# Attention: how the sums over the values are divided and brought into the order of the last layer

## The reference

```python
x = x + 0.5 * ffn(layernorm(x))
x = x + attention(layernorm(x))
x = x + 0.5 * ffn(layernorm(x))

def attention(x):                       # 16 heads of 16 features, scale = 16 ** -0.25
    xd = (x @ W_down).reshape(b, t, 16, 16)
    keys, queries = (einsum('bthk,hik->bthi', xd, w) * scale for w in (tokeys, toqueries))
    values = einsum('bthk,hik->bthi', xd, tovalues)
    attn = softmax(einsum('bqhs,bkhs->bhqk', queries, keys), axis=-1)
    out = einsum('bhqk,bkhs->bqhs', attn, values).reshape(b, t, 256)
    return out @ W_unify + b_unify
```

## Time and profile before

| | us |
|---|---|
| median of 3 runs | 2948.91 (2944.68 to 2953.52) |
| profiled execution, its own time | 2942.43 |
| its span in the profile | 2940.3 |
| TensorE busy | 2753.6 (94%) |
| VectorE busy | 2133.7 (73%) |
| ScalarE busy | 1863.4 (63%) |
| GpSimd busy | 539.7 (18%) |
| mean granted TensorE clock | 0.968 of full |

### The profile page before, as it was taken

How to read it: one execution, slowest core, us unless ns; L and a number is a source line. 1 busy time by engine, 2 the same in 40 slices (tenths; PEclk the granted TensorE clock), 3 DMA queues, 4 the chain that set the end, 5 groups by cost and what they waited for, 6 DMA issues and landing times. The chain is left out here.

```text
span 2940.3 us, 49181 instructions
## 1 busy us (share of the span) xinstructions
PE 2753.6 (94%) x17263; PEld 1663.3 (57%) x17263; DVE 2133.7 (73%) x3460; ACT 1863.4 (63%) x3505; POOL 539.7 (18%) x498
## 2 busy tenths in 40 slices
PE   5999999867999999999999999999999679999997
PEld 3799998853334343333343443333433369999886
DVE  6554456748888888898898888888897465445664
ACT  5444455634777777777777777777777454544564
POOL 3354124520000000000000000000000145421353
PEclk9999999977999999999999999999999889999998
DMA  5221113415033132131230330321220412111242
GB/s 170 65 57 43 43 59 113 130 38 89 15 58 69 25 65 47 38 60 36 48 73 15 59 67 23 67 45 37 47 43 8 149 47 72 52 48 43 89 140 66
DMA packets 159668, 180.69 MB, mean 61 GB/s; under 512 B 31816, under 2 KB 129296, under 8 KB 159504
## 3 DMA queue, kind: packets, MB, share of 16 engines
q1 hardware_dynamic: 151312, 167.99, 23.4%
q0 software_dynamic: 8192, 10.57, 1.2%
HBM read 96.46 MB, written 30.49 MB: 43 GB/s over the span
## 5 line engine op out<-in xcount | busy, mean ns | idle before, releaser
L1518 DVE TENSOR_REDUCE at_mxc<-at_pb 128x2 f32<-128x1024 f32 x1024 | 1222.7, 1219 | 159.6 <-PE at_pb L1335 152.0
L1448 ACT ACTIVATE at_ex<-at_pd 128x512 f32<-128x512 f32 x2048 | 1092.9, 598 | 355.0 <-PE at_pd L1346 346.4
L768 DVE TENSOR_TENSOR f_ml_hl<-f_ml_h,f_ml_hh 128x512 fp32r<-128x512 f32 (+1 forms) x384 | 265.2, 692 | 441.1 <-ACT f_ml_hh L844 382.8
L1346 PE MATMUL at_pd<-at_qa,at_ka 50*128 50x512 f32 x2048 | 573.4, 466 | 3.3 <-ACT at_ex L1448 2.5
L1346 PEld LDWEIGHTS at_pd<-at_qa,at_ka 50*128 50x128 f32 x2048 | 255.8, 185 | 526.9 <-issue 271.3
L1355 PE MATMUL at_po<-at_ex,at_va 128*32 128x512 f32 x4096 | 547.1, 606 | 0.2 <-ACT at_ex L1448 0.2
L841 ACT ACTIVATE f_ml_h<-f_ml_pL,b1T 128x512 f32<-128x512 f32 (+1 forms) x384 | 243.6, 634 | 449.9 <-PE f_ml_pL L895 373.6
L1335 PE MATMUL at_pb<-at_ka,at_qa 48*128 48x512 f32 x2048 | 441.8, 450 | 16.0 <-DVE at_mxc L1518 10.7
L910 PE MATMUL f_ml_pA<-f_wh,f_ml_hh 128*128 128x256 f32 (+1 forms) x1408 | 408.8, 290 | 0.0
L912 PE MATMUL f_ml_pA<-f_wl,f_ml_hh 128*128 128x256 f32 (+1 forms) x1408 | 401.3, 285 | 0.0
L913 PE MATMUL f_ml_pA<-f_wh,f_ml_hl 128*128 128x256 f32 (+1 forms) x1408 | 401.3, 285 | 0.0
(11 more groups left out here) (124 smaller groups left out, 2658.9 us busy)
## 6 DMA issues: line engine op xcount, KB each, us to landing
f_wraw<-in_L_ffn_w SPq DMA_DIRECT2D x128, 256.0 KB, 2.7
at_qa<-at_parts SPq DMA_DIRECT2D x384, 64.0 KB, 2.4
at_ka<-at_parts SPq DMA_DIRECT2D x384, 64.0 KB, 2.4
f_ro_xr<-in_L_attn_x SPq DMA_DIRECT2D x16, 512.0 KB, 3.6
f_ml_xr<-in_L_attn_x SPq DMA_DIRECT2D x16, 512.0 KB, 3.9
x<-f_ml_yo SPq DMA_DIRECT2D x16, 512.0 KB, 3.8
at_xr<-x SPq DMA_DIRECT2D x16, 512.0 KB, 5.2
at_xres<-x SPq DMA_DIRECT2D x8, 1024.0 KB, 6.6
```

What stands on the lines that cost most here:

```text
L768: eng.tensor_tensor(hl[h % RING][:, 0:w], h32[h % 2][:, 0:w], hh[h % RING][:, 0:w].bitcast(F32), ALU.subtract).then_inc(s_lo.sem, 1)
L1346: eng.matmul(pd[n % RING][:, :], ka[g][rows, p, kt * P:(kt + 1) * P], qa[g][rows, qh, p, :], start=True, stop=True).then_inc(s_full.sem, 1)
L1448: eng.activation(ex[t % 2][:, j, :], pd[n % RING][:, :], ACT.Exp).then_inc(s_free[n % RING].sem, 1)
L1518: eng.tensor_reduce(mxc[:, t // NT, kh, t % NT::NT], pb[kh][:, :].rearrange("p (e k) -> p e k", e=2), AX.X, ALU.max).then_inc(s_mx.sem, 1)
```

## The change

The fifteen columns of zeros in `va` become ones. So `po` and `os_` hold the total of a head on sixteen rows, 16 to 31, right under its sixteen sums. `heads_out`, a new function on SyncE, takes the place of the first transposes: for each of the four heads of a half it copies the 16 rows of sums to the rows of `aT` where the last layer wants them, and the 16 rows of totals to the same rows of a new tile `den`. These are 8 DMAs for each half of a group, 512 in all. VectorE's `values_out` waits for those of the half before.

When both groups of a column half c (two groups give the 128 rows of `aT[:, f, c]`) are in, VectorE takes the reciprocals of `den` in four pieces of 128 x 128, one a step: for f = 0 in steps 10 to 13 of groups 1 and 3, for f = 1 in steps 2 to 5 of the group behind. That is 16 pieces a batch, 128 in all. GpSimd multiplies `aT` by `den` in one 128 x 512 instruction (`divide`), 32 in all. The side products "f" and "aT" are gone, with VectorE's and ScalarE's work behind them. The four "u" of a batch stand in steps 1, 2, 9 and 15 of group 0 of the next batch (before: steps 5 and 6 there, and 13 and 14 of group 3); in the last batch two are in steps 14 and 15 of group 3 and two behind the end.

```diff
-        OUT = lambda f: [("aT", f, 0), ("aT", f, 1), ("u", f, 0), ("u", f, 1)]
+        OUT = lambda f: [("u", f, 0), ("u", f, 1)]
-            table = {1: ("f", 1), 9: ("f", 0), 4: ("mx", 1), 12: ("mx", 0)}
-            if g == 0 and not prev:
-                del table[1]
+            table = {4: ("mx", 1), 12: ("mx", 0)}
             if g == 0 and prev:
-                table.update(zip((2, 3, 5, 6), OUT(1)))
-            if g == 3:
-                table.update(zip((10, 11, 13, 14), OUT(0)))
+                table.update(zip((1, 2, 9, 15), OUT(0) + OUT(1)))
+            if g == 3 and last:
+                table.update(zip((14, 15), OUT(0)))
...
+            def heads_out(ring, b, g, qh, read):
+                eng.wait_ge(s_o.sem, s_o.at(2 * unit(b, g) + qh + 1))
+                if b > 0:
+                    eng.wait_ge(s_full.sem, s_full.at(ring.full(read)))
+                if b > 0 or g > 1:
+                    eng.wait_ge(s_dv.sem, s_dv.at(4 * b + 2 * (g // 2) + qh - 1))
+                for j in range(GH):
+                    r0, r1 = HS * (GH * (g % 2) + j), VW * j
+                    eng.dma_start(aT[r0:r0 + HS, qh, g // 2, :], os_[r1:r1 + HS, :]).then_inc(s_nd.sem, 16)
+                    eng.dma_start(den[r0:r0 + HS, qh, :], os_[r1 + HS:r1 + 2 * HS, :]).then_inc(s_nd.sem, 16)
...
                 def step(self, b, par, g, t, coming, tiles, done, a, side, ahead, last):
+                    if t == NT:
+                        heads_out(self.ring, b, g, 0, self.read[0])
+                    if t == 0 and (b or g):
+                        heads_out(self.ring, *((b, g - 1) if g else (b - 1, 3)), 1, self.read[1])
...
                 else:
                     f, half = a.at
+                    eng.wait_ge(s_dv.sem, s_dv.at(4 * a.b + 3 + f))
                     for i in range(2):
                         q = (2 * half + i) * P
                         for c in range(DT):
-                            mm = eng.matmul(bank[:, i * D:(i + 1) * D], aT[:, c, q:q + P], w.wu[:, c, :],
+                            mm = eng.matmul(bank[:, i * D:(i + 1) * D], aT[:, f, c, q:q + P], w.wu[:, c, :],
                                             start=(c == 0), stop=(c == DT - 1))
...
             def values_out(b, g, t):
                 eng.wait_ge(s_pv.sem, s_pv.at(ST * unit(b, g) + t + 1))
+                eng.wait_ge(s_nd.sem, s_nd.at(16 * 2 * GH * (2 * unit(b, g) + t // NT)))
                 eng.tensor_copy(os_[:, :], po[:, :]).then_inc(s_o.sem, 1)
+
+            def reciprocals(b, c, f, q):
+                n = 4 * (4 * b + 2 * c + f)
+                at = slice(q * P, (q + 1) * P)
+                if q == 0:
+                    eng.wait_ge(s_nd.sem, s_nd.at(16 * 2 * GH * (2 * unit(b, 2 * c + 1) + f + 1)))
+                eng.reciprocal(den[:, f, at], den[:, f, at]).then_inc(s_rc.sem, 1)
...
-                elif a.kind == "f":
-                    eng.wait_ge(s_full.sem, s_full.at(ring.full(a.n)))
-                    u = unit(a.b, a.g)
-                    v = bank[:, :].rearrange("p (t j s) -> p t j s", t=4, j=GH)
-                    eng.reciprocal(rec[:, :, :], v[:, :, :, HS]).then_inc(s_rc.sem, 1)
...
-                        eng.memset(v[:, :, :, HS + 1:VW], 0.0)
-                        eng.memset(v[:, :, :, HS:HS + 1], 1.0).then_inc(s_one, 1)
+                        eng.memset(v[:, :, :, HS:VW], 1.0).then_inc(s_one, 1)
...
+                    if g % 2 and NT + 2 <= t < NT + 6:
+                        reciprocals(b, g // 2, 0, t - NT - 2)
+                    if g % 2 == 0 and 2 <= t < 6 and (b or g):
+                        reciprocals(*((b, 0) if g else (b - 1, 1)), 1, t - 2)
...
                 def end(self, sides):
+                    for q in range(4):
+                        reciprocals(NBAT - 1, 1, 1, q)
...
+            def divide(b, c, f):
+                eng.wait_ge(s_rc.sem, s_rc.at(4 * (4 * b + 2 * c + f + 1)))
+                eng.tensor_tensor(aT[:, f, c, :], aT[:, f, c, :], den[:, f, :], ALU.mult).then_inc(s_dv.sem, 1)
...
+                    if g % 2 and t == NT + 5:
+                        divide(b, g // 2, 0)
+                    if g % 2 == 0 and t == 5 and (b or g):
+                        divide(*((b, 0) if g else (b - 1, 1)), 1)
```

More of the change, by code:

```diff
@@ L1118, in attention @@
         s_rc = S("s_rc")
+        s_nd = S("s_nd")
+        s_dv = S("s_dv")
         s_xl = S("s_xl")
@@ L1183, in __init__ @@
                         self.phase(do, b, b % 2, g, prev=b > 0, last=b == NBAT - 1)
-                do.end([self.place(task, NBAT - 1, 1, 3) for task in [("f", 1)] + OUT(1)])
+                do.end([self.place(task, NBAT - 1, 1, 3) for task in OUT(1)])
             def place(self, task, b, par, g):
@@ L1223, in _ @@
         def _(eng):
-            for s in (*s_xr, *(x for two in s_ld for x in two), *s_mr, s_xl, *s_st):
+            for s in (*s_xr, *(x for two in s_ld for x in two), *s_mr, s_nd, s_xl, *s_st):
                 s.open(eng)
@@ L1312, in step @@
                         store_out(self.ring, a)
+                        self.read[a.at[0]] = a.n
                 def end(self, sides):
-                    for a in sides[3:]:
+                    heads_out(self.ring, NBAT - 1, 3, 1, self.read[1])
+                    for a in sides:
                         store_out(self.ring, a)
@@ L1450, in side_out @@
             def side_out(ring, a):
-                if a.kind in ("f", "u"):
+                if a.kind == "u":
                     return
@@ L1544, in side_out @@
             def side_out(ring, a):
-                if a.kind not in ("qk", "mx", "f", "u"):
+                if a.kind not in ("qk", "mx", "u"):
                     return
@@ L1654, in end @@
                 def end(self, sides):
-                    pass
+                    divide(NBAT - 1, 1, 1)
             Walk(eng, Do())
```

33 lines of the change are left out of this document (9 added, 24 removed).

## The result

The changed kernel takes 2963.43 us (median of 20 runs, 2950.22 to 2970.12) against 2946.17 (20 runs, 2939.0 to 2953.52) for the kernel before on the same chip: a ratio of 1.0056 with an interval of 1.0045 to 1.0066. It is slower by about half a per cent, some 16 us. The forecast was 2958.

The account below looks back on a forecast made before the run. TensorE sets the time, with only a seventh of VectorE free. Terms -45.3 + 40.8 + 3.1 + 5.9 + 7.7 = +12.2 us give 2954.6 or 2961.1 by baseline; the middle, 2958, was forecast, range 2924 to 2988.

Parts of the forecast that it names:

- The saving of 45.3 us: In the attention's steps: TensorE loses 63 "f" and 30 "aT", saving 45.3 us if VectorE lets it.
- One reciprocal at 0.95 us: On VectorE: one 128 x 128 reciprocal takes 0.95 us, from a fixed 148 ns and 6.25 ns an element.
- the cheap one: Rival: a VectorE reciprocal takes 0.37 us, so the kernel gets faster, 2923 us; chance 0.12.
- the one of eight beats: Rival: each element of VectorE's reciprocal takes eight beats, 1.18 us in all; +22, 2980 us; chance 0.17.
- Group 0, steps 0 to 7, 29.4 us: Batches 1 to 6: VectorE's work makes these steps 29.4 us, a loss of 3.7 a batch.
- Groups 1 and 2: Batches 1 to 6: group 1 changes by -0.1 us, group 2 by -1.0; last batch: 0.9 us longer each.
- Group 3, with a wait of 0.6 us each: Steps 10 to 13: VectorE's work and a 0.6 us DMA wait lose 2.2 a batch; group changes by -3.0.
- Behind the last step, +7.7: After the steps: 12.9 us from the copy to the first "u" instead of 5.2, 7.7 more, uncovered.
- The last batch's group 3, -1.0: Last group of the last batch: its length changes by -1.0 us.
- The rival of a smaller backlog: Rival: VectorE's backlog is smaller, 1 us less in each of 20 places, -20, 2938 us; chance 0.16.

Follow-up runs that it names:

- e2_small: Changed kernel with reciprocals of 128 x 16 instead of 128 x 128, most totals not inverted: 2910.37 us, ratio 0.9883.
- e6_dmas: Kernel before plus only the 512 new DMAs, to scratch in HBM, and the wait of `values_out` for them: 2946.37 us, ratio 1.0013.
- e8_late: Changed kernel with reciprocals of groups 1 and 3 one step later, GpSimd's product behind them, except in the very last group: 2956.6 us, ratio 1.0038.
- e12_nofill: e11_all without the filler transposes: 2939.97 us, ratio 0.9992.
- e4_moved: Changed kernel with group 0's reciprocals moved to steps 8 to 11, one "u" to step 13, one "xd" to group 1: 2954.77 us, ratio 1.0011.
- e1_fill: Changed kernel with filler, four unread transposes in each of steps 5 to 13 of the last batch's last group: 2959.23 us, ratio 1.0053.
- e11_all: Changed kernel with group 0's reciprocals at steps 8 to 11, groups 1 and 3's a step later, filler, tail DMAs on two queues: 2936.42 us, ratio 0.9963.
- e3_gap: Kernel before with the last group's "f" and "aT" put off to steps 11 to 13, "u" to 14 and 15: 2948.88 us, ratio 1.0012.
- a2_again: Changed kernel, unaltered, run once more on another chip: 2974.05 us, ratio 1.0064.
- e5_moved_fill: e4_moved with the filler transposes of e1_fill, on the same chip: 2954.24 us, ratio 0.9998.

## Why the prediction was right, and where it was not

The forecast was a sum of +12.2 us, with the time set by VectorE's new work. The ratio gives about +16, the profiled executions +21.8.

- *The saving of 45.3 us*: right. Steps that held "f" or "aT" are plain, 2.61, where VectorE lets them be, and e2_small has them so in group 3 but for the step that waits for the DMAs. Without the reciprocals' work the kernel is some 34 us under before (e2_small), with the tail and the clock's falls in it.
- *One reciprocal at 0.95 us*: right, 0.936 measured. This decides between the rivals: the cheap one (0.37, or anything under 0.82) and the one of eight beats (1.18) are both out. The Trainium skill ("VectorE: DVE Perf Modes", on the fixed hardware budget) gives the divide a repeat count of 8. The runs don't bear that out as a time: 936 less 239 ns over 112 more elements are 6.2 ns each, six beats of 1.04. The measurement decides.
- *Group 0, steps 0 to 7, 29.4 us*: 28.9 measured (1103.64 to 1132.54); the whole group +4.8 where +5.0 stood. In batches 1 and 6, two blocks at half clock add 1.5 us to it.
- *Groups 1 and 2*: within 0.3 us in batches 1 to 6, 0.5 and 0.3 less than forecast in the last.
- *Group 3, with a wait of 0.6 us each*: the mean of the six is 45.0, -2.9 against -3.0. The waits were forecast at 0.6 in each batch; batches 0 and 6 have none, batches 1 to 5 have 0.68 to 1.24, and a landing took 1.9 us (median) instead of 2.4. In batch 2 the wait shows in step 12 (4.14 us instead of 3.10), and steps 13 to 15 take 2.98 to 3.08; the prediction had named steps 10 to 13. e6_dmas shows that SyncE's work alone costs little, e8_late that group 3 is 0.5 to 2.1 us shorter where the reciprocals needn't wait.
- *Behind the last step, +7.7*: +7.0.
- *The last batch's group 3, -1.0*: this is the term that failed. It measured +9.0. The prediction added TensorE's steps at full clock throughout, and had no term for the clock at all. In the one group behind which no scores are made, TensorE idles for 0.45 us a step in steps 5 to 8 before the change as well; the change takes away the "f" and "aT" of steps 9 to 11 and so leaves nine such steps in a row. In some executions the clock falls to 1.2 GHz somewhere in them (at step 8 in three profiles, at 6 in e12_nofill, at 13 in e4_moved) and stays there until a "u" runs, six steps at 1.46 us each in the profile after. The filler shows that TensorE's thin load is needed for it: 43.6 against 54.2 us (e1_fill), 43.7 against 56.5 (e11_all and e12_nofill), and no fall there in any of four profiles that have it, against five of six without.
- *The rival of a smaller backlog* fell: the losses came out as large as counted.

The profiled execution lies 9.6 us above the sum (21.8 against 12.2), and this one term accounts for 10.0. The others miss by +2.3 (groups but the last, mostly the half clock in group 0), -0.7 (behind the steps) and -1.6 (elsewhere); that they cancel to a tenth is luck. The median lies 5 us above the forecast; that it is less fits a fall that comes in some executions only, but how often it comes in the changed kernel itself wasn't counted (both its profiles have it).

What stays open: why the clock falls in some executions and not in others of the same kernel. e3_gap's profile, with thin steps and nothing else of the change, shows no fall; e8_late's, with all steps of the last group as after the change, shows none either; three profiles (of the changed kernel twice, and e2_small) show the same six steps slow. What precedes the fall doesn't tell them apart: in steps 5 to 7 of the last group TensorE's load is the same in all of them, and in the kernel before too. The runs tell how often, not when. Also open is e1_fill's ratio, which moved by 0.0003 only, where five falls of 12 us in twelve executions would have it move by 0.0017 (5/12 x 12 / 2946): each of the two intervals is wider than that. The slow blocks in group 3 of batches 1 to 6 are clearer. In the six profiles whose reciprocals stand in steps 10 to 13 (after, a2_again, e1_fill, e2_small, e4_moved, e5_moved_fill), 14 of these groups have such a block, and in each of the 14 the first reciprocal had waited 0.53 to 1.78 us for its DMA. Twelve others waited 0.65 to 1.38 and have none. In the four profiles with the reciprocals a step later no reciprocal waits there, and none of the groups has a slow block. e2_small is among the six, so the wait brings them even where the reciprocal's own work is small. So in these traces the wait always stands ahead of them, but doesn't always bring one; the four ran on other chips than the experiments among the six.
